# A recommender's forward pass: one by-hand pair less, block copies of three pairs shared, a shorter index chain

## What is computed

```python
x = relu(dense @ W0 + b0); x = relu(x @ W1 + b1); dense_out = relu(x @ W2 + b2)
emb = vmap(lambda t, idx: t[idx])(tables, sparse)   # [2048, 26, 64], one row of each of 26 tables a sample
gram = einsum('bid,bjd->bij', emb, emb)             # [2048, 26, 26]
interact = gram[:, TRIU_I, TRIU_J]                  # 325 products of different fields
features = concatenate([dense_out, interact], axis=1)
return features @ Wt + bt                           # [2048, 256]
```

## Time and profile before

| | us |
|---|---|
| median of 3 runs | 529.29 (527.62 to 530.14) |
| the profiled execution, its own time | 523.91 |
| its span, first to last instruction | 522.1 |
| POOL busy | 378.3 (72%) |
| PE busy | 300.1 (57%) |
| DVE busy | 253.1 (48%) |
| ACT busy | 14.0 (3%) |

### The profile page before, as it was taken

One profiled execution on the slowest core, in us unless ns is written; L12 is line 12 of the kernel. 1 busy time (PEld: TensorE's weight loads), 2 busy tenths in 40 slices (PEclk: granted clock), 3 DMA queues, 4 the chain that ended last, 5 costly groups with the idle time before them and its releaser, 6 DMA issues.

```text
span 522.1 us, 9067 instructions
## 1 busy us (share of the span) xinstructions
PE 300.1 (57%) x1752; PEld 240.0 (46%) x1752; DVE 253.1 (48%) x656; ACT 14.0 (3%) x37; POOL 378.3 (72%) x407
## 2 busy tenths in 40 slices
PE   2714762757576695857768181361724619065787
PEld 1503541546465574646647171350613418054675
DVE  4354533246638455563745555071551825438442
ACT  2000000000000000000000000000000000000422
POOL 5777777777777777777777777777777777777750
PEclk9976575777677776777777766575755756558879
DMA  7222224232222223232322223232222222221210
GB/s 111 28 29 29 29 46 95 32 38 28 38 29 39 29 29 39 28 40 29 39 28 29 38 28 39 28 39 27 31 28 38 30 38 28 37 31 36 38 31 11
DMA packets 25398, 18.78 MB, mean 36 GB/s; under 512 B 15095, under 2 KB 18905, under 8 KB 25324
## 3 DMA queue, kind: packets, MB, share of 16 engines
q0 software_dynamic: 12800, 13.13, 17.5%
q1 hardware_dynamic: 6356, 2.49, 5.2%
q10 hardware_dynamic: 6186, 2.58, 4.8%
HBM read 15.25 MB, written 2.10 MB: 33 GB/s over the span
## 4 chain that ended last, share of the span: by engine, by line
POOL 63%; issue 22%; PE 7%; DMA 4%; DVE 3%; POOLq 0%; DVEq 0%
POOL emb L319 63%; DMA emb<-in_L_rec_tables_dram,row_idx 4%; PE gram_ps L656 3%; PE mlp_ps L668 2%; DVE gram L234 2%; PE mlp_ps L616 1%; DMA raw_idx<-n_r_sparse_features_dram 1%; PE rowsT_ps L632 0%; PE mlp_ps L664 0%; DVE embT L224 0%; DVE embT L211 0%; DVE out_sb L445 0%; DVE embT L221 0%; DVE wrap L365 0%; POOLq L313 0%
## 5 line engine op out<-in xcount | busy, mean ns | idle before, releaser
L319 POOL DMA_INDIRECT emb<-in_L_rec_tables_dram,row_idx x374 | 353.0, 944 | 117.6 <-issue 113.8
L234 DVE COPY gram<-gram_ps 32x96 f32<-32x96 f32 x480 | 155.8, 325 | 100.9 <-PE gram_ps L656 91.2
L656 PE MATMUL gram_ps<-embT 64*128 64x100 f32 x1024 | 94.8, 355 | 24.6 <-DVE gram L234 11.6
L632 PE MATMUL rowsT_ps<-ident,emb 128*128 128x128 f32 x187 | 36.9, 333 | 122.6 <-DMA emb<-in_L_rec_tables_dram,row_idx 109.4
L656 PEld LDWEIGHTS gram_ps<-embT 64*128 64x128 f32 x1024 | 88.8, 264 | 34.0 <-issue 34.0
L632 PEld LDWEIGHTS rowsT_ps<-ident,emb 128*128 128x128 f32 x187 | 24.7, 166 | 134.3 <-issue 133.7
L211 DVE COPY embT<-rowsT_ps 128x512 f32<-128x512 f32 (+1 forms) x60 | 47.5, 851 | 73.1 <-PE rowsT_ps L632 72.7
L581 PE MATMUL mlp_ps<-h,w_sb 128*128 128x256 f32 x128 | 47.3, 549 | 36.2 <-DVE h L420 36.2
L668 PE MATMUL mlp_ps<-w_gram,gram 128*128 128x256 f32 x224 | 67.7, 468 | 0.1
L668 PEld LDWEIGHTS mlp_ps<-w_gram,gram 128*128 128x128 f32 x224 | 56.4, 252 | 12.5 <-issue 0.5
L581 PEld LDWEIGHTS mlp_ps<-h,w_sb 128*128 128x128 f32 x128 | 36.2, 291 | 47.9 <-DVE h L420 40.0
(11 more groups left out here) (38 smaller groups left out, 47.1 us busy)
## 6 DMA issues: line engine op xcount, KB each, us to landing
by_hand<-in_L_rec_tables_dram SPq DMA_DIRECT2D x1024, 0.2 KB
by_hand<-in_L_rec_tables_dram ACTq DMA_DIRECT2D x1024, 0.2 KB
emb<-in_L_rec_tables_dram,row_idx POOLq DMA_INDIRECT x376, 3.4
out_dram<-out_sb ACTq DMA_DIRECT2D x16, 128.0 KB, 9.6
w_gram<-w_tri SPq DMA_DIRECT2D x3, 192.0 KB
w_sb<-in_L_rec_W_dram SPq DMA_DIRECT2D x1, 512.0 KB
emb<-in_L_rec_tables_dram,last_idx POOLq DMA_INDIRECT x24, 2.5
raw_idx<-n_r_sparse_features_dram SPq DMA_DIRECT2D x2, 182.0 KB, 4.4
```

Of the source, the lines that this page charges most:

```text
L234: last = copy(by_quad[FP * g:FP * (g + 1), t0:NS, :, half * HG:(half + 1) * HG, s], gram_ps[FP * s:FP * (s + 1), :, :, src:src + SQ * (NS ...
L319: nc.gpsimd.indirect_dma_start(emb[:, m % PR, k, u, :], None, tables_v[:, :], bass.IndirectOffsetOnAxis(ap=row_idx[:, 2 * m + u, k:k + 1], ...
L632: last = nc.tensor.transpose(rowsT_ps[c % 2][:, k - ks.start, :, :], rows.rearrange("p u e -> p (u e)"), ident[:, :])
L656: last = nc.tensor.matmul(gram_ps[:, u, a, 0:SQ * (F - 1)], samples.rearrange("p s f -> p (s f)"), samples[:, :, 1:F], start=True, stop=True)
```

## The change

Three edits:

- `BY_HAND` loses its last entry, 14. Pair 14's two gathers of k = 12 are issued by POOL like the others; SP and ACT fetch seven pairs' rows by hand, 896 each instead of 1024.
- `SHARED` begins at pair 13 instead of 14: ACT copies half of the blocks of pairs 13, 14 and 15.
- The raw indices of the lower 64 partitions are stored one element further on than those of the upper 64, so one strided view gives even fields below and odd fields above. Wrap, clamp and sum, five operations before, are two on all 128 partitions, and with the table's base it is three. `row_idx`, `wrap`, `wrapped` and `field_base` get another layout for it; `capped` goes.

```diff
@@ -58,7 +58,7 @@
     LAST = len(CHUNKS) - 1
 
 
-    BY_HAND = [2, 4, 5, 7, 9, 10, 12, 14]
+    BY_HAND = [2, 4, 5, 7, 9, 10, 12]
     HAND_K = NK - 1
     LOADED = 32
     ROW = EMB * 4
@@ -71,7 +71,7 @@
     LAST_CHUNKS = [None, (0, 0, 4), (0, 4, LK), (1, 0, 4), (1, 4, 5), (1, 5, LK)]
     HALF_DONE = [3, 6]
 
-    SHARED = range(LAST_PAIR - 1, NP)
+    SHARED = range(LAST_PAIR - 2, NP)
 
     SPARE = [4, 3, 5]
 
@@ -105,11 +105,12 @@
             return ctx.enter_context(nc.semaphore(name))
 
         ident = sb("ident", [P, P])
-        raw_idx = sb("raw_idx", [P, 2, NP, F], i32)
-        wrap = sb("wrap", [P, NU, NK])
-        capped = sb("capped", [P, NU, NK])
-        wrapped = sb("wrapped", [P, NU, NK])
-        field_base = sb("field_base", [P, 1, NK], i32)
+
+
+        raw_idx = sb("raw_idx", [P, 2, NP * F + 1], i32)
+        wrap = sb("wrap", [P, 2, NP, NK])
+        wrapped = sb("wrapped", [P, 2, NP, NK])
+        field_base = sb("field_base", [P, 1, 2, NK], i32)
 
 
 
@@ -121,7 +122,7 @@
         hand_row = sb("hand_row", [NU, US, 2])
         hand_off = sb("hand_off", [NU, 2 * US], u32)
 
-        row_idx = sb("row_idx", [P, NU, NK], u32)
+        row_idx = sb("row_idx", [P, 2, NP, NK], u32)
         last_raw = sb("last_raw", [P, 4, F], i32)
         last_wrap = sb("last_wrap", [P, 4, LK])
         last_capped = sb("last_capped", [P, 4, LK])
@@ -262,10 +263,11 @@
         @block.sync
         def _(sp):
 
-            sp.dma_start(raw_idx[0:US, :, 0:2, :], sparse_v[:, :, 0:2, :]).then_inc(idx_in[0], 16)
+            sp.dma_start(raw_idx[0:US, :, 1:2 * F + 1], sparse_v[:, :, 0:2, :].rearrange("s h t f -> s h (t f)")
+                         ).then_inc(idx_in[0], 16)
             for x in range(2):
-                sp.dma_start(raw_idx[x * US:(x + 1) * US, :, 2:NP, :], sparse_v[:, :, 2:NP, :]).then_inc(
-                    idx_in[1], 16)
+                sp.dma_start(raw_idx[x * US:(x + 1) * US, :, 2 * F + 1 - x:NP * F + 1 - x],
+                             sparse_v[:, :, 2:NP, :].rearrange("s h t f -> s h (t f)")).then_inc(idx_in[1], 16)
             for h in range(2):
                 sp.dma_start(hand_raw[h * NP:(h + 1) * NP, :, :], sparse_v[:, h, :, 2 * HAND_K:2 * HAND_K + 2].rearrange(
                     "s t x -> t s x")).then_inc(hand_idx_in, 16)
@@ -296,7 +298,7 @@
         def _(pool):
 
             for x in range(2):
-                nc.gpsimd.iota(field_base[x * US:(x + 1) * US, 0, :], pattern=[[2 * VOCAB, NK]],
+                nc.gpsimd.iota(field_base[x * US:(x + 1) * US, 0, :, :], pattern=[[0, 2], [2 * VOCAB, NK]],
                                base=x * VOCAB, channel_multiplier=0).then_inc(base_ready, 1)
 
             pool.wait_ge(base_ready, 2)
@@ -318,7 +320,7 @@
                         for u in range(2):
                             nc.gpsimd.indirect_dma_start(
                                 emb[:, m % PR, k, u, :], None, tables_v[:, :],
-                                bass.IndirectOffsetOnAxis(ap=row_idx[:, 2 * m + u, k:k + 1], axis=0),
+                                bass.IndirectOffsetOnAxis(ap=row_idx[:, u, m, k:k + 1], axis=0),
                             ).then_inc(rows_in[m % PR][c], 16)
 
 
@@ -334,7 +336,7 @@
                     for u in range(2):
                         nc.gpsimd.indirect_dma_start(
                             emb[:, LAST_PAIR % PR, HAND_K, u, :], None, tables_v[:, :],
-                            bass.IndirectOffsetOnAxis(ap=row_idx[:, 2 * LAST_PAIR + u, HAND_K:HAND_K + 1], axis=0),
+                            bass.IndirectOffsetOnAxis(ap=row_idx[:, u, LAST_PAIR, HAND_K:HAND_K + 1], axis=0),
                         ).then_inc(last_rows_in[i], 16)
                     continue
                 half, k0, k1 = chunk
@@ -354,28 +356,28 @@
 
             for part, (u0, u1) in enumerate(PARTS):
                 dve.wait_ge(idx_in[part], 32)
-                halves = [(slice(x * US, (x + 1) * US),
-                           raw_idx[x * US:(x + 1) * US, :, u0 // 2:u1 // 2, x:F:2].rearrange("s h t k -> s t h k"))
-                          for x in range(2)]
-
-                def by_unit(buf, rows):
-                    return buf[rows, u0:u1, :].rearrange("s (t h) k -> s t h k", h=2)
-
-                for rows, raw in halves:
-                    nc.vector.tensor_scalar(by_unit(wrap, rows), raw, 0.0, float(VOCAB), ALU.is_lt, ALU.mult)
-                    last = nc.vector.tensor_scalar(by_unit(capped, rows), raw, float(VOCAB - 1), None, ALU.min)
-                last.then_inc(idx_step, 1)
+                def part_of(buf):
+                    return buf[:, :, u0 // 2:u1 // 2, :].rearrange("s h t k -> s h (t k)")
+
+                raw = raw_idx[:, :, u0 // 2 * F + 1:u1 // 2 * F + 1:2]
+                nc.vector.tensor_scalar(part_of(wrap), raw, 0.0, float(VOCAB), ALU.is_lt, ALU.mult).then_inc(idx_step, 1)
                 dve.wait_ge(idx_step, 2 * part + 1)
-                nc.vector.tensor_tensor(wrapped[:, u0:u1, :], capped[:, u0:u1, :], wrap[:, u0:u1, :],
-                                        ALU.add).then_inc(idx_step, 1)
+                nc.vector.scalar_tensor_tensor(
+                    out=part_of(wrapped), in0=raw, scalar=float(VOCAB - 1), in1=part_of(wrap), op0=ALU.min,
+                    op1=ALU.add).then_inc(idx_step, 1)
                 dve.wait_ge(idx_step, 2 * part + 2)
                 if part == 0:
                     dve.wait_ge(base_ready, 2)
-                dst = row_idx[:, u0:u1, :]
-                nc.vector.scalar_tensor_tensor(
-                    out=dst, in0=wrapped[:, u0:u1, :], scalar=0.0,
-                    in1=field_base[:, :, :].to_broadcast([P, u1 - u0, NK]), op0=ALU.max,
-                    op1=ALU.add).then_inc(idx_ready if part == 0 else later_ready, 1)
+                    nc.vector.scalar_tensor_tensor(
+                        out=part_of(row_idx), in0=part_of(wrapped), scalar=0.0,
+                        in1=field_base[:, :, :, :].rearrange("p a t k -> p a (t k)").to_broadcast([P, 2, 2 * NK]),
+                        op0=ALU.max, op1=ALU.add).then_inc(idx_ready, 1)
+                else:
+                    for h in range(2):
+                        last = nc.vector.scalar_tensor_tensor(
+                            out=row_idx[:, h, u0 // 2:u1 // 2, :], in0=wrapped[:, h, u0 // 2:u1 // 2, :], scalar=0.0,
+                            in1=field_base[:, :, 0, :].to_broadcast([P, (u1 - u0) // 2, NK]), op0=ALU.max, op1=ALU.add)
+                    last.then_inc(later_ready, 1)
 
 
             dve.wait_ge(hand_idx_in, 32)
@@ -463,7 +465,7 @@
 
                 nc.vector.scalar_tensor_tensor(
                     out=last_row[:, :, :], in0=last_wrapped[:, :, :], scalar=0.0,
-                    in1=field_base[:, :, 0:2 * LK:2].to_broadcast([P, 4, LK]), op0=ALU.max,
+                    in1=field_base[:, :, 0, 0:2 * LK:2].to_broadcast([P, 4, LK]), op0=ALU.max,
                     op1=ALU.add).then_inc(hand_idx_step, 1)
                 dve.wait_ge(hand_idx_step, 6)
                 for x in range(SQ):
@@ -500,7 +502,8 @@
 
         @block.scalar
         def _(act):
-            act.dma_start(raw_idx[US:P, :, 0:2, :], sparse_v[:, :, 0:2, :]).then_inc(idx_in[0], 16)
+            act.dma_start(raw_idx[US:P, :, 0:2 * F], sparse_v[:, :, 0:2, :].rearrange("s h t f -> s h (t f)")
+                          ).then_inc(idx_in[0], 16)
             act.dma_start(x_sb[:, :, :], dense_v).then_inc(x_in, 16)
             act.dma_start(w0_sb[:, :], w0).then_inc(mlp_w_in, 16)
             with nc.allow_non_contiguous_dma(reason="bias columns"):
```

## The result

| | before | changed |
|---|---|---|
| median, lowest to highest of 7 runs each, us | 528.53 (526.01 to 530.14) | 523.65 (523.36 to 523.73) |
| ratio, 95% interval | | 0.9914 [0.9891, 0.9937] |
| profiled execution, own time, us | 523.91 | 523.56 |
| its span, us | 522.1 | 521.5 |

The change is 4.9 us faster, and its times lie within 0.4 us of each other where those of before lie 4 apart. The two profiled executions differ by 0.35 us only. The time that was gained is hardly to be seen between them; that is the key to what the prediction missed.

What follows compares the result with a forecast made beforehand. Bound: PE and DVE behind pair 13's late data, from one DMA engine overloaded by by-hand rows, with POOL's gathers 4 us behind. +2.50 - 0.36 - 3.92 = -1.78 us, so 529.29 becomes 527.5; range 521.8 to 530.2, own range 526 to 529.

Steps and rivals of the forecast that it cites:

- each place named: Signs of being right: by-hand end, pair 13's landing, gather pace and times, last transpose, 11.8 us behind it, pair 14's wait gone.
- PE's lateness: At the last gather PE takes up data about 4 us late, behind pair 13's late data; its going was counted as -3.92 us.
- a difference that stays: The profiled execution's own time, 523.91, lies 5.4 us under the median; taken as lasting, so the gain came off 529.29.
- the stated range: Range for the changed kernel's time, from 521.8 to 530.2 us.
- longer-tail rival: Timed runs have more backlog on the overloaded DMA engine, 26 us instead of 20.57; all 5.4 us go: 522.1, chance 0.27.
- One by-hand pair less: Two more gathers on POOL's row, +2.50 us; backlog drained before 412, so pair 13 lands in 2.4 to 3.3 us.
- Shared copies: Pair 13's copies split between DVE and ACT: alone about 3.0 us earlier on PE, in the change counted at nothing.
- The index chain: At the head, two steps instead of more precede the last operation; the first gather starts 0.36 us earlier, range 0 to 0.86.
- Less backlog: Pair 13 lands sooner in timed runs: no gain at 18.8 us; 3.9 us sooner than 20.57 gives 531.4, slower; chance 0.13.
- PE's clock falls in the last stage: More PE waits between 488 and 508 halve its clock in the last stage, +5.7 us: 533.2, chance 0.07.
- the clock rows: Trace rows: 32 product matmuls take 3.74 us at granted clock 0.50, 2.05 at 1.00; the last stage ran at 1.00.
- It does not do what it says: The backlog outlasts pair 13's gathers, so only pair 13's shared copies pay, 3.0 us: about 526, chance 0.03.

Runs made afterwards that it cites:

- before_again: The kernel before, unchanged, for a second profile: 526.74 us, ratio 0.9991 to before.
- head: The kernel before with only the shorter index chain, eight by-hand pairs and copies shared from pair 14 on: 527.62 us, ratio 0.9996 to before.
- hand6: The change with six by-hand pairs, 12 also dropped, so two gathers more than the change: 525.9 us, ratio 0.9965 to before.
- hand8_fill: The change with eight by-hand pairs, plus 5, 5 and 3 unused matmuls in PE's waits: 520.85 us, ratio 0.9884 to before.
- fill: The kernel before with 13 unused matmuls where PE would wait, nine in pair 14 and four in the last pair: 523.24 us, ratio 0.9925 to before.
- no_head: The change without the index chain edit: seven by-hand pairs, copies shared from pair 13 on: 524.21 us, ratio 0.9933 to before.
- hand8: The change with eight by-hand pairs, so only shared copies and the short index chain against before: 523.09 us, ratio 0.9927 to before.
- after_fill: The change with 18, 7 and 4 unused matmuls in PE's waits: 524.41 us, ratio 0.9935 to before.
- hand7: The kernel before with only 14 taken off the by-hand list: 523.65 us, ratio 0.9931 to before.
- share3: The kernel before with only pair 13's block copies also shared by DVE and ACT, eight by-hand pairs: 523.13 us, ratio 0.9919 to before.
- early7: The change with seven by-hand pairs that include 14 and leave out 2: 524.18 us, ratio 0.9930 to before.
- half14: The change with pair 14's first unit fetched, its second by a gather: 521.85 us, ratio 0.9898 to before.

## Why the prediction was right, and where its size was off

**The mechanism held at each place named but one.** By-hand issue ends near 391 (389.5), pair 13 lands within 4 us (2.8), the 5.62 us of pair 14 are gone (PE waits there for gathers), the last transpose starts within 0.3 of its landing (0.14), 11.8 us remain behind it (11.85). The exception is the last gather, which starts at 507.03 and not at 505.9, although the first came at 4.92 and not at 5.06. POOL's row decides the end, by 0.18 us of PE's waiting in the profiled execution where the prediction had 0.9. The Trainium skill, DMA: Bandwidth & Descriptors, in the section on why a DMA increments its semaphore by 16, says that HWDGE gives a transfer the lowest-numbered of the engines, as many as its shape is split over, and that an SWDGE transfer is complete only when all sixteen have posted. By this, copies that run on one engine all meet on the same one, and a gather is complete only when its share there is through; the trace agrees, with 6.0% of sixteen engines' time in the by-hand queues until 463 before, and 20.57 us to landing that fall to 2.8.

**The failed step: the size of PE's lateness.** In the sum it was 3.92 us, from one profile of before. Two further profiles of the same tail show 5.9 (before_again, own time 526.5) and 7.6 (head, own time 528.2), with the same late data. It was the profiled execution that was unusual, quicker than any timed one. The prediction took the 5.4 us between it and the median as "a difference that stays", a constant between profile and timed runs; but the timed runs' own spans are longer by about as much (1.75 to 2.2 us lie between time and span in each), so no such offset exists. The 5.4 us were PE's slower tail, which stopped counting when pair 13's data came 17 us earlier. The forecast's own range, 526 to 529, was missed; that 523.65 lies in the stated range is owed to the longer-tail rival, whose cause was wrong, and so in part to luck.

**The sum anew**, from executions nearer to the median. The last gather starts at 504.29 in before_again and at 507.03 in the change, +2.74: two gathers +2.50; the first gather about -0.5 (4.92 for 5.4, of which 0.38 is the chain and the rest earlier index loads); the third and fourth gather +0.4, beside DVE's index work; about +0.3 of pace and what is left over. PE's lateness goes: -7.6 as in head, -5.9 as in before_again. That is -4.9 and -3.2, where -4.9 was measured between the medians. The 7.6 is one profile of a kernel that differs from before in its index chain; no profile of before itself near 528.5 was taken. Against the first profile of before, the last gather came 3.30 later where the prediction had 2.14: the +0.4 had no term in its sum, and the pace of 1.249, taken as without spread, is 1.250 over the whole row of before_again.

**Part by part.** *One by-hand pair less*: right in kind and in its price; hand6 and hand8_fill both show 2.3 to 2.4 for two gathers against 2.50, with first gathers that also differ by up to 0.5. *Shared copies*: "count it at nothing" is right inside the change; alone they are worth 4.3 to 4.8, of which the trace shows 2.7 at PE's wait before pair 14's third chunk. Whether the rest is a shorter tail at the lower clock, or the spread of the runs, is not shown. *The index chain*: 0.36 was forecast, from first to last operation it is 0.48 for 0.86, so 0.38. The second part of it, which was said to end long before its rows are needed, gives about as much back in this execution, with the third gather and the fourth 0.4 us longer; no term of the sum had a price for that.

The changed kernel's head (DVE, then POOL):

```profile
3.31 0.19 DVE L363 TENSOR_SCALAR wrap<-raw_idx 128x52 f32<-128x52 int32 x1 [2.03 <-DMA raw_idx<-n_r_sparse_features_dram]
3.54 0.21 DVE L365 SCALAR_TENSOR_TENSOR wrapped<-raw_idx,wrap 128x52 f32<-128x52 int32 x1
3.79 0.21 DVE L371 SCALAR_TENSOR_TENSOR row_idx<-wrapped,field_base 128x52 uint32<-128x52 f32 x1
...
4.92 1.10 POOL L321 DMA_INDIRECT emb<-in_L_rec_tables_dram,row_idx  x1 [3.23 <-DVE row_idx L371]
...
7.58 1.26 POOL L321 DMA_INDIRECT emb<-in_L_rec_tables_dram,row_idx  x1 [0.30 <-issue]
```

**The rivals.** *The longer tail* came nearest in size, 522.1, on a wrong cause: it put the 5.4 us on more backlog, and before_again shows the backlog the same (19.84 us). Its time was right because any cause of a late PE would go with the change. *Less backlog*, the slower side, did not occur: the late landing was 19.6 to 20.8 us in the profiles named above that have eight by-hand pairs, never under 18.8; and behind it PE's lateness over POOL's row was larger in before_again and head than in the first profile, not smaller. *PE's clock falls in the last stage* did not occur in the change either, which is granted 1.00 to 0.99 from 503.9 to its end; it did in the profile of fill, to 0.72 for 1.3 us, not to 0.50 for 5.7. (PE's gaps ahead of the last stage were not all under 1 us, as it said: a wait of 2.60 us ends at 496.22, and one of 1.04 follows.) The prediction had the clock rows before it and looked for the danger only in the change's last stage; the same fall, ahead of that stage, was already in the kernel before and made its tail long. The change does not take it away: pair 14's last layer still takes 4.67 us, at 0.67. But PE starts on pair 13 17 us sooner, so this slow work ends 0.18 us ahead of POOL's last data. *It does not do what it says* fell with the 2.8 us.

**Why the three remedies do not add up.** Fewer by-hand rows, shared copies and fillers each take 4 to 5 us out of before, and two or three of them together (no_head, hand8, after_fill) no more. Behind the late PE stands POOL's row of gathers. With fewer by-hand rows the profiles reach it (hand7, no_head, the change), and so does that of fill; with shared copies alone PE is still late, by 5.4 us in the profile of share3 and by 2.3 in that of hand8, but POOL's row is two gathers shorter there. Only what also shortens POOL's row goes on: hand8_fill keeps the eighth by-hand pair, covers the late data with shared copies and the clock with fillers, and ends 2.8 us below the change.

## What to carry to other kernels

Compare a profiled execution's own time with the timed runs before summing from it: if it lies below all of them, the profile shows an untypical case, and the difference has a place in the trace that one should look for in a second profile. When an engine's waits lower its granted clock, the wait costs again in the work behind it, so cutting the wait, shortening what precedes it, or filling it with unused matmuls can be worth the same. Many one-row copies can build up a backlog, here with about one DMA engine's time of sixteen, and gathers then land up to 20 us late, until some 18 us after the copies' issue ended. A remedy that leaves the slow stage as it is can still pay in full, if it lets that stage start earlier than what comes last.

## What was not expected of the hardware

- Beside DVE's index operations on 128 x 364 elements a gather took 1.25 to 1.26 us instead of 0.94, in the profiles of head, hand8, early7 and the change, where it started 0.1 us into the second operation. In hand8_fill and after_fill, where it started elsewhere beside the same operations, it took 0.94 to 0.95, in hand6 and half14 1.05 to 1.11. Why is not shown.
- POOL's pace differs between executions of one kernel: 1.2489 us a gather in the first profile of before, 1.2504 in the second, 0.6 us over the program.
- The first index loads released DVE at 3.31 us in one profile and at 4.08 in another, and the whole row of gathers moves with them.
- Thirteen unused matmuls of PE shortened the program by 4.9 us.
